# Variances and factors of the late norms on VectorE as three-operand instructions

## The reference

```python
x = x + _L0_attn_ref(_layernorm(x), Wq, bq, Wk, bk, Wv, bv, Wo, bo, gamma, beta)
x = x + _L0_ffn_ref(_layernorm(x), w_router, w_block)

def _L0_attn_ref(x, ...):                  # 16 heads of 8
    q = elu(x @ Wq + bq) + 1 ; k = elu(x @ Wk + bk) + 1 ; v = x @ Wv + bv
    k = k / sqrt(sum(k * k) + EPS)         # per head
    out = ((q k^T) v) @ Wo + bo            # no softmax, so k^T v can be made first
    y = x + out
    return (y - mean(y)) / sqrt(var(y) + EPS) * gamma + beta

def _L0_ffn_ref(x, w_router, w_block):
    scores = x @ w_router                  # one per row
    _, top_idx = top_k(scores, 768)        # 768 of the 1024 rows of a sequence
    processed = gelu(x[top_idx] @ w_block)
    return x.at[top_idx].set(processed)
```

## Time and profile before

| what | value |
|---|---|
| median of 3 runs | 91.68 us (91.58 to 91.70) |
| profiled execution, its own time | 91.51 us |
| span of that execution | 89.8 us |
| VectorE busy | 80.9 us (90%), 258 instructions |
| TensorE busy | 79.9 us (89%) |
| ScalarE busy | 66.9 us (75%) |
| GpSimd busy | 52.8 us (59%), 79 instructions |
| TensorE clock granted | 0.992 of full on average |

### The profile page before, as it was taken

One profiled execution on the slowest core, in us unless ns is written; L12 is line 12 of the kernel. 1 busy time (PEld: TensorE's weight loads), 2 busy tenths in 40 slices (PEclk: granted clock), 3 DMA queues, 4 the chain that ended last, 5 costly groups with the idle time before them and its releaser, 6 DMA issues.

```text
span 89.8 us, 2397 instructions
## 1 busy us (share of the span) xinstructions
PE 79.9 (89%) x816; PEld 68.4 (76%) x816; DVE 80.9 (90%) x258; ACT 66.9 (75%) x186; POOL 52.8 (59%) x79
## 2 busy tenths in 40 slices
PE   4998689999999999999999599999999797999700
PEld 1335656976797997999999599999998797779600
DVE  4368999999797897999999999999999999999960
ACT  5003599998999996753539799999799696998700
POOL 5265885989992997659770979769838400000000
PEclk9999999999999999999999999999999999999996
DMA  0899969970999999900000000000000000348456
GB/s 24 233 256 319 280 168 319 290 189 7 143 127 140 139 143 136 112 10 0 0 0 0 0 7 0 0 4 7 0 4 0 0 7 10 107 121 236 138 149 180
DMA packets 18113, 8.99 MB, mean 100 GB/s; under 512 B 819, under 2 KB 18102, under 8 KB 18102
## 3 DMA queue, kind: packets, MB, share of 16 engines
q1 hardware_dynamic: 13232, 6.49, 26.7%
q0 software_dynamic: 4160, 2.10, 21.5%
q10 hardware_dynamic: 710, 0.26, 1.1%
HBM read 4.66 MB, written 2.10 MB: 75 GB/s over the span
## 4 chain that ended last, share of the span: by engine, by line
PE 46%; DVE 41%; issue 4%; ACT 3%; DVEq 1%; POOL 1%; ACTq 0%
DVE beats L918 11%; PE bank L1219 7%; PE bank L1211 7%; PE bank L1152 6%; DVE xb_sb L886 5%; DVE x_sb L941 5%; DVE bn L893 4%; PE bank L1252 4%; PE bank L1228 4%; PE bank L1253 4%; PE bank L1188 3%; PE bank L1271 3%; DVE beats L927 2%; DVE bn L818 2%; DVE x_sb L853 2%
## 5 line engine op out<-in xcount | busy, mean ns | idle before, releaser
L918 DVE TENSOR_SCALAR beats<-s_row,s_col 128x1024 bf16<-128x1024 f32 (+7 forms) x32 | 15.5, 541 | 0.0
L595 ACT ACTIVATE norm_sb<-xb_sb,shift,gain 128x128 f32<-128x128 f32 x32 | 13.2, 507 | 2.7 <-DVE shift L847 2.7
L1252 PE MATMUL bank<-M_sb,qT 128*128 128x128 f32 x64 | 12.5, 277 | 0.0
L1253 PE MATMUL bank<-back,hT 128*128 128x128 f32 x64 | 12.4, 275 | 0.0
L413 POOL TENSOR_TENSOR r<-var,minus_half 128x4 f32<-128x4 f32 x8 | 8.1, 1025 | 5.8 <-DVE var L833 5.5
L400 POOL TENSOR_TENSOR k_sb<-k_sb,k_rnorm 128x512 f32<-128x512 f32 x8 | 9.3, 1252 | 2.7 <-DVE k_rnorm L801 2.7
L426 POOL TENSOR_TENSOR r<-var,minus_half 128x4 f32<-128x4 f32 x8 | 9.1, 1194 | 2.9 <-DVE var L839 2.9
L1252 PEld LDWEIGHTS bank<-M_sb,qT 128*128 128x128 f32 x64 | 9.7, 192 | 0.2 <-ACT M_sb L558 0.2
L1253 PEld LDWEIGHTS bank<-back,hT 128*128 128x128 f32 x64 | 9.7, 192 | 0.0
L588 ACT ACTIVATE x_sb<-bank,r 128x128 f32<-128x128 f32 x32 | 9.2, 383 | 0.2 <-DVE s_col L901 0.2
L1219 PEld LDWEIGHTS bank<-w_c,hT 128*128 128x128 f32 x56 | 6.9, 192 | 2.1 <-ACT hT L513 1.1
(11 more groups left out here) (132 smaller groups left out, 216.7 us busy)
## 6 DMA issues: line engine op xcount, KB each, us to landing
xb_sb<-in_L_attn_x_dram SPq DMA_DIRECT2D x4, 512.0 KB, 6.8
xb_sb<-beta_sb POOLq DMA_DIRECT2D x4, 512.0 KB, 8.4
x_sb<-in_L_attn_x_dram SPq DMA_DIRECT2D x7, 256.0 KB, 5.2
out_dram<-x_sb SPq DMA_DIRECT2D x7, 256.0 KB, 2.3
x_sb<-in_L_attn_x_dram SPq DMA_DIRECT2D x2, 128.0 KB, 2.7
out_dram<-x_sb SPq DMA_DIRECT2D x1, 128.0 KB, 2.4
out_dram<-x_sb ACTq DMA_DIRECT2D x1, 128.0 KB, 2.5
w_sb<-in_L_attn_Wq_dram ACTq DMA_DIRECT2D x1, 64.0 KB, 2.5
```

Of the source, the lines that this page charges most:

```text
L595: last = nc.scalar.activation(norm_sb[:, t], xb_sb[:, t], ACT.Identity, bias=shift3[:, t:t + 1], scale=gain3[:, t:t + 1])
L918: nc.vector.tensor_scalar(beats[:, b % 2, J, P * J:T * P], s_row[:, b, P * J:T * P], s_J, None, ALU.is_le).then_inc(beats_done, 1)
L1252: nc.tensor.matmul(o, qT[:, u, t * P:(t + 1) * P], M_sb[:, b], start=True, stop=False)
L1253: last = nc.tensor.matmul(o, hT[:, u, t * P:(t + 1) * P], back[:], start=False, stop=True)
```

## The change

Three constant columns are added, filled in `constants()` behind `eps_col`: `attn_eps`, `ln_eps` and `one_col`. The two variances and the factor, which had one tensor and two numbers as operands (`tensor_scalar`), take the tensor, one number and a constant column stretched over the 4 columns (`scalar_tensor_tensor`). Numbers, places in the lists and semaphores stay as they are. The lines of the kernel after stand some lines lower than before.

```diff
+        attn_eps, ln_eps, one_col = sb("attn_eps", [P, 1]), sb("ln_eps", [P, 1]), sb("one_col", [P, 1])
...
                 nc.vector.memset(eps_col[:], ATTN_EPS)
+                nc.vector.memset(attn_eps[:], ATTN_EPS)
+                nc.vector.memset(ln_eps[:], LN_EPS)
+                nc.vector.memset(one_col[:], 1.0)
...
             def variances2(u):
...
-                nc.vector.tensor_scalar(var2[:, t0:t1], m2, 1.0 / D, ATTN_EPS, ALU.mult, ALU.add).then_inc(var2_done, 1)
+                nc.vector.scalar_tensor_tensor(out=var2[:, t0:t1], in0=m2, scalar=1.0 / D, in1=attn_eps[:].to_broadcast([P, TH]), op0=ALU.mult,
+                                               op1=ALU.add).then_inc(var2_done, 1)
...
             def variances3(u):
...
-                nc.vector.tensor_scalar(var3[:, t0:t1], m2, 1.0 / D, LN_EPS, ALU.mult, ALU.add).then_inc(var3_done, 1)
+                nc.vector.scalar_tensor_tensor(out=var3[:, t0:t1], in0=m2, scalar=1.0 / D, in1=ln_eps[:].to_broadcast([P, TH]), op0=ALU.mult,
+                                               op1=ALU.add).then_inc(var3_done, 1)
...
             def affine3(u):
...
-                nc.vector.tensor_scalar(gain3[:, t0:t1], r3[:, t0:t1], 1.0, None, ALU.add)
+                nc.vector.scalar_tensor_tensor(out=gain3[:, t0:t1], in0=r3[:, t0:t1], scalar=1.0, in1=one_col[:].to_broadcast([P, TH]),
+                                               op0=ALU.mult, op1=ALU.add)
```

## The result

The kernel after takes 91.86 us (median of 17 runs, 91.31 to 92.14), the kernel before beside it 91.45 us (17 runs, 91.18 to 91.84): 1.0036 times as long, 95% interval 1.0021 to 1.0050. The loss is 0.3 to 0.4 us (0.41 between the medians, 0.33 by the ratio), small but clear of zero.

What follows compares the result with a forecast made beforehand. VectorE, busy 80.9 of 89.8 us, and TensorE hold the chain. Profiled 91.51 us with terms 0 + 0 + 0 - 0.05 gave 91.46; the median of runs lies 0.17 above, so 91.6 us, range 90.95 to 91.9.

Steps and rivals of the forecast that it cites:

- The own cost of the forms: 24 small VectorE instructions: 0.07 us from start to start in either form, so 0, bounds -0.24 and +0.24 us.
- The wait of 0.16 us at 32.95 us: Variance held by GpSimd's key multiply; removing it gives 0, since VectorE then idles 0.49 us for TensorE's matrix.
- The wait of 0.60 us: Half 2's variance at 41.30 us, held by GpSimd's multiply: mostly stays, -0.05 us taken between 0 and -0.60; chance 0.50.
- The small gain that I allowed for: Half 2's variance at 41.30 us: -0.05 us if it waits for GpSimd's reads alone, not its last write.
- Rival 1: Half 2's variance at 41.30 us passes GpSimd's multiply, all VectorE behind 0.60 us earlier: 91.08 us; chance 0.37.
- What I named as next late: Places checked behind half 2's variance; tightest y_stats of half 3 with 0.2 us to spare, so the whole 0.60 comes through.
- The three fills: Behind eps_col's fill at the start: hidden by VectorE's 1.42 us wait for x, so 0; up to 0.18 us uncovered.
- Rival 2: From 55.20 us and two later places, a GpSimd root's write delays a VectorE comparison: 92.0 us, slower; chance 0.09.

Runs made afterwards that it cites:

- e1: Kernel before with the 24 small instructions in three-operand form, reading existing columns, no new column or fill: 91.56 us, ratio 1.0005.
- e8: Kernel after with the half 2 variance taking its third operand from PSUM and y_gamma waiting for it by a semaphore: 90.76 us, one run.
- e10: Kernel before with half 2's variance behind y_gamma and the fills of eps_col and minus1 moved from VectorE to GpSimd: 92.45 us, ratio 1.0092.
- e14: Kernel before with only the fills of eps_col and minus1 moved from VectorE to the head of GpSimd's list: 92.72 us, ratio 1.0158.
- e3: Kernel before with the variance of half 2 put behind y_gamma of half 2 in VectorE's list: 90.76 us, ratio 0.9902.
- e11: Kernel before with the variance of half 2 put behind y_gamma of half 2, run again for a closer interval: 90.78 us, ratio 0.9919.
- e2: Kernel before with the three new columns and their fills on VectorE, read by nothing, old forms kept: 91.78 us, ratio 1.0021.
- e9: Kernel before with three new columns filled by the last three instructions of VectorE's list: 91.67 us, ratio 1.0021.
- e5: Kernel before with the three new columns allocated and no fill: 91.29 us, ratio 0.9993.
- e7: Kernel before with the three new columns filled at the head of GpSimd's list, read by nothing: 91.45 us, ratio 1.0013.

## Why the prediction failed

The range, 90.95 to 91.9, holds the 91.86 us, but it was centred on no change, and the change is a loss of 0.36% with an interval clear of it. Step by step:

- **The own cost of the forms, 0: right within its bounds of 0.24 us.** e1 gives 1.0005 (0.9982 to 1.0027) and starts are 0.07 us apart in both; the traces show 0.02 to 0.04 us of loss over all 24.
- **The wait of 0.16 us at 32.95 us, 0 in either case: untested.** It stayed at 0.32 us in all, so what would follow without it was not seen.
- **The wait of 0.60 us stays, -0.05: right in what it says.** The variance takes 0.77 us. The small gain that I allowed for, from reads that end sooner than the last write, did not come: it ends 0.02 us behind the multiply's end, as the old form ended 0.01 behind. The reason that I chose this end, the second tensor in SBUF, is shown by e8 (0.15 us with one of two tensors in PSUM), and the masks of e10 and e14 fit it. The rule of the Trainium skill ("SBUF — State Buffer", section "Who interferes with whom"), that two SBUF inputs contend with a GpSimd instruction that reads SBUF, agrees with both. It does not agree with the roots: they too read two tensors in SBUF, and the new factor and the shift, with two SBUF tensors each, take 0.15 us inside them (46.25 and 46.32 us of after).
- **Rival 1's price, -0.60: right.** It didn't happen, but e3 and e11 took the wait away in another way and got 0.60 us in the trace, 0.7 to 0.9 in time. What I named as next late (root 2, y_stats of half 3, the score rows) did not come late.
- **The three fills, 0: wrong, and this is the step that failed.** I asked what covers them on VectorE, and inside the span that holds: 0.01 us apart, ahead of a wait of 1.40 us. Their price without cover was set too high, since they overlap: the wait shrank by 0.02 us and not by 0.1 to 0.2. But the sum was made on "span 89.8 and 1.7 around it", with the 1.7 taken as fixed. It is not: it was 2.12 us. e2 and e9 show the fills as the cause, e5 and e7 that neither the tiles nor GpSimd's list do it. The term should have been +0.36 us for three fills, which gives 91.68 + 0.36 = 92.04 on the runs shown and 91.45 + 0.36 = 91.81 on those measured later, where 91.86 was found. No row of before could have given this number. Why VectorE's list changes the time outside the span stays open.
- **Rival 2, a root ahead of a comparison: did not happen.** The comparisons behind the factors start as before: VectorE of after stays 0.12 to 0.17 us behind before throughout. The kernel did come out slower, but not by this. What can cost a microsecond is a mask or a comparison that comes just behind the start of GpSimd's sum (e10, e14), and for that the change moved nothing.

## What to carry to other kernels

Weigh an added instruction twice: on its engine's timeline, and in the time of the run that the span does not hold; compare time less span over all runs of both kernels, since in before's 29 runs it ranges over 0.11 us where the time ranges over 1.0. When a small VectorE instruction ends each time with a GpSimd instruction beside it, suspect that it waits for that. Here another form that reads two tensors from SBUF was no cure, but putting it behind a neighbour that reads PSUM was, and one swapped line gave 0.8%. And where a VectorE instruction starts only 0.3 us ahead of such a GpSimd instruction, a change far ahead of it, even two fills moved at the start, can cost a microsecond.

## What had not been expected of the hardware

- Three fills more in VectorE's list, of 0.06 us each and run while nothing waits, cost 0.36 us outside the span, at the head or the end of the list; one cost 0.13, six 0.27, two fewer gain nothing, three more on GpSimd nothing. The one run with three fills and a wait more lost nothing outside.
- A three-operand instruction over 4 columns takes 0.77 us beside GpSimd's multiply over 512 when both tensors are in SBUF, and 0.15 us when one is in PSUM. Beside GpSimd's root over 4 elements (1.0 us) it is not held: the factor at 46.25 us takes 0.15 us while two roots run.
- A bf16 mask of 0.41 us takes 1.44 when it starts 0.12 us behind GpSimd's sum.
